# A routed feed-forward stage whose first tiles are fetched in four steps instead of two

## Chip, cores and metric

One core of one Trainium2 chip. The time is device microseconds of one execution; the median of three runs of the kernel before is 184.93 us (184.1 to 185.01). Everything below names lines of the kernel before.

## What is computed

Three layers, each closed by a residual sum and a layer norm, on 1,024 tokens (4 sequences of 256) of width 256, in fp32.

```python
x = _layernorm(x + attn(x, Wq, Wk, Wv, Wo))        # 16 heads that share one softmax
x = _layernorm(x + xattn(x, token_ids, ctx))       # expert = token_id // 3125, of 4
x = _layernorm(x + ffn(x, Wr, br, Wg, Wu, Wd))     # expert = argmax of a router, of 4

# ffn: each token goes to one expert e
h = silu(x @ Wg[e]) * (x @ Wu[e])                  # 256 -> 1024
y = (h @ Wd[e]) * top_probability                  # 1024 -> 256
```

Layers two and three both send each token to one of four experts, so the tokens are sorted by expert twice. The change is about the second sort, between layer two and layer three.

## The kernel before

**Layer two** works on ten tiles of 128 rows (T = 10). Its results are normalised in four groups (GROUPS: tiles 0 to 2, 3 and 4, 5 and 6, 7 to 9). For each group VectorE picks the expert of every row (`choose`), TensorE adds up how many earlier rows go to each expert (`rank`, into the PSUM tile `pR`), VectorE turns that into a row number (`place`), and GpSimd scatters each tile's rows to a buffer in DRAM, `scr2`, by that number (`scatter2`). There every expert has a region of eight blocks of 128 rows.

**Layer three** works on items (q, t): a quarter q of the hidden width and a tile t. A tile is one block of one expert. The last tile (JOINT = 9) joins two half blocks of up to 64 rows, of two experts, in one. There are 4 x 10 items, and in the first quarter tile and item have the same number. For an item j TensorE transposes the rows of a tile (`ftx`, L819), multiplies by the gate and up weights (`fup`, L833; each fp32 product is made from three fp32r products of high and low parts, L574), transposes the hidden rows (`fth`, L877) and multiplies by the down weights (`fdown`, L885). ScalarE copies the high parts (`fxhi`, `fhhi`) and does the silu (`fsilu`), VectorE makes the low parts (`fxlo`, `fhlo`), the product of gate and up (`fhidden`) and adds up the result (`fsum`). Each engine goes through a list written out in program order; for a usual i it is `ftx(i+1)`, `fup(i)`, `fth(i-1)`, `fdown(i-2)`. Nothing overtakes on an engine.

**Which block is a tile** is found out at run time. A block that is sure to be full can be worked on before all rows are scattered: with n tiles routed at least (128 n - 4 x 127) / 128 blocks, rounded up, are full. The kernel before uses this once. After seven routed tiles (ROUTED = 7, the first three groups) VectorE looks for three full blocks (EARLY = 3; `early_whole`, `early_table`, L1364 to L1371), which become tiles 0 to 2. The other full blocks, the larger rests and the smaller rests get tiles 3 to 9 after all ten tiles (`late_counts`, `late_blocks`, `late_rows`, L1378 to L1391).

VectorE hands on two kinds of numbers by semaphore. `row_table` (L1350) tells SyncE's DMA queue where a tile begins in `scr2`; SyncE reads each number into a register (`first_row`, L390) and starts the load (`routed_row`, L393). `tables` (L1361) tells TensorE which expert's weights a tile needs; TensorE reads that into a register at the head of each `fup` (L830). `late_offsets` (L1393) ends with `joint_expert`, the two experts of the joint tile; SyncE waits for it (L416), reads two registers, loads their weights of the first quarter in fp32 (`load_w32`, L409: two DMAs of 768 KB each) and then the two halves of the joint tile's rows (L419 to L421).

**SyncE's order before**, around the change (L395 to L425): wait for `row_table` 1, three register reads, wait for seven scatters, load tiles 0 to 2; wait for `row_table` 2, three reads, wait for the last three scatters, load tiles 3 to 5; wait for `row_table` 3, read and load tiles 6, 7 and 8; wait for `row_table` 4, `load_w32(0)`, the joint rows; then the weight chunks 7 to 15 (`load_chunk`, 768 KB each), each when a staging slot is free.

**The weights of the next quarter** are split beside the items: ScalarE copies a piece of 128 x 512 as high part (L964), GpSimd subtracts (L487). `share` (L312) says how many of 12 pieces go beside each item, and item 10, the first of the second quarter, waits for all twelve. Chunk 7 holds the last three pieces of that quarter.

Between the layers TensorE runs products of ones that nobody reads (`idle_products`, L582: 20 before the last `rank`, 6 behind it, 2 behind `ftx(0)` and `ftx(1)`).

Of the kernel before, what the change touches and what calls it, by code (L numbers as in the profile page):

```python
# [16 lines left out]
P = 128  # L17
# [6 lines left out]
E = 4  # L24
# [30 lines left out]
LATE = 2 * EARLY  # L55
SORTED = BATCH - 1
ROUTED = 7
# [10 lines left out]
def route_kernel(nc, aw, xT_in, x_in, ids_in, wr_in, br_in, ctx_in, ctxn_in, wffn_in, out):  # L68
# [3 lines left out]
    with ExitStack() as ctx:  # L72
# [57 lines left out]
        base8 = sb("base8", [P, T + 2, E + 1], BF16)  # L130
# [11 lines left out]
        slot_of = sb("slot_of", [P, BLOCKS])  # L142
        shift = sb("shift", [P, BLOCKS + 1])
# [74 lines left out]
        pR = bank[6][:, 0:(T + 2) * (E + 1)].rearrange("p (t e) -> p t e", e=E + 1)  # L218
# [12 lines left out]
        d_scat1, d_scat2, d_out = [sem(f"d_scat1_{i}") for i in range(2)], [sem(f"d_scat2_{i}") for i in range(2)], sem("d_out")  # L231
# [80 lines left out]
        share = [[0, 0, 1, 1, 2, 2, 2, 2, 2, 0], [1, 1, 2, 1, 2, 1, 2, 1, 1, 0], [1, 1, 2, 1, 2, 1, 2, 1, 1, 0]]  # L312
# [9 lines left out]
        CONSTS = 27  # L322
# [8 lines left out]
        def _(sp):  # L331
# [99 lines left out]
        def _(pool):  # L431
            def const(ins):
# [30 lines left out]
                         allow_small_or_imprecise_dtypes=True))  # L463
            const(g.memset(cap[:], HIGH))
            const(g.iota(base8[:, :, 0:E], pattern=[[0, T + 2], [REGION // P, E]], base=0, channel_multiplier=0,
# [62 lines left out]
            def scatter2(t):  # L528
                pool.wait_ge(slot_ready, GROUP_OF[t] + 1)
                pool.wait_ge(x2_ready, t + 1)  # L530
                g.indirect_dma_start(out=scr2, out_offset=bass.IndirectOffsetOnAxis(ap=slot2[:, t:t + 1], axis=0),  # L531
                                     in_=buf[:, t, :], in_offset=None, bounds_check=E * REGION - 1,
                                     oob_is_err=False).then_inc(d_scat2[t // ROUTED], 16)

# [16 lines left out]
            for t in range(ROUTED, T):  # L551
                scatter2(t)
# [18 lines left out]
        def _(pe):  # L571
# [207 lines left out]
            def rank(n):  # L779
                a, b = GROUPS[n]  # L780
                pe.wait_ge(mask_ready, n + 1)
                mm(pR[:, a:b, :], below[:], m2[:, a:b, :], start=False, stop=False, skip_group_check=True)
                for s in range(a, b):
                    end = T + 2 if s < ROUTED else T + 1
# [30 lines left out]
            idle_products(20)  # L815
            rank(3)
            idle_products(6)
# [81 lines left out]

            pe.wait_ge(tables, 2)  # L900
            ftx(0)
            for i in range(len(items) + 2):
                if i == EARLY:
                    fth(i - 1)
                    fdown(i - 2)
                    ftx(i)
                    ftx(i + 1)
                    fdown(i - 1)
                    pe.wait_ge(tables, 3)
                    fup(i)  # L910
                else:
                    if i + 1 < JOINT and i + 1 != EARLY:
                        ftx(i + 1)
                    if i == 0:
                        idle_products(2)
                    if i < len(items):
                        fup(i)
                    if i + 1 == JOINT:
                        ftx(i + 1)
                    if 1 <= i <= len(items):  # L920
                        fth(i - 1)
                    if i >= 2 and i != EARLY + 1:
                        fdown(i - 2)
# [3 lines left out]
        def _(act):  # L927
# [138 lines left out]
            for t in range(ROUTED, T):  # L1066
                norm2(t)

# [27 lines left out]

            fxhi(0)
            for i in range(len(items) + 4):
                if i == EARLY:
                    fhhi(i - 1)  # L1100
                    fxhi(i)
                    fxhi(i + 1)
                    fsilu(i)
                else:
                    if i + 1 < JOINT and i + 1 != EARLY:
                        fxhi(i + 1)
                    if i < len(items):
                        fsilu(i)
                    if i + 1 == JOINT:
                        fxhi(i + 1)  # L1110
                    if 1 <= i <= len(items):
                        fhhi(i - 1)
                if i - 4 >= len(items) - T:
                    norm_row(i - 4 - (len(items) - T))
                if i < len(items):
                    for k in pieces_beside(i):
                        split(k)
# [3 lines left out]
        def _(dve):  # L1121
# [242 lines left out]
            def early_whole():  # L1364
                dve.wait_ge(r_done, GROUP_OF[ROUTED - 1] + 1)
                step(v.tensor_tensor(out=by_expert(whole[:]), in0=per_block(pR[:, T + 1, 0:E]), in1=ends[:], op=ALU.is_ge))

            def early_table():
                running(nth[:], whole[:])
                block_table(0, EARLY, 0, nth[:], BLOCKS)  # L1370
                row_table_of(0, EARLY)  # L1371

            def early_offsets():
                dve.wait_ge(row_table, 1)
                expert_table(0, EARLY)
                offset_table(0, EARLY)

            def late_counts():  # L1378
                counts = per_block(pR[:, T, 0:E])
                step(v.tensor_tensor(out=by_expert(by_size[:, 0, :]), in0=counts, in1=begins_half[:], op=ALU.is_gt))  # L1380
                step(v.tensor_tensor(out=by_expert(by_size[:, 1, :]), in0=counts, in1=begins[:], op=ALU.is_gt))
                step(v.tensor_tensor(out=by_size[:, 1, :], in0=by_size[:, 1, :], in1=by_size[:, 0, :], op=ALU.subtract))
                step(v.tensor_tensor(out=by_size[:, 0, :], in0=by_size[:, 0, :], in1=flags[:, 0, :], op=ALU.subtract))
                running(nth_by_size[:], by_size[:].rearrange("p s j -> p (s j)"))

            def late_blocks(a, b):
                block_table(a, b, a - EARLY, nth_by_size[:], 2 * BLOCKS)

            def late_rows(a, b):
                wrapped(a, b)  # L1390
                row_table_of(a, b)  # L1391
# [24 lines left out]
            for i in range(T):  # L1416
# [27 lines left out]
                if i == 9:  # L1444
                    shifts(2)
                    choose(2)
                    residual_sum(7)
            place(2)
            residual_moments(7)
            early_whole()  # L1450
            early_table()
# [78 lines left out]
            for i in range(len(items) + 3):  # L1530
                if i == EARLY:
                    fhlo(i - 1)
                    fxlo(i)
                    fxlo(i + 1)
                    fhidden(i)
                else:
                    if 1 <= i and i + 1 < JOINT and i + 1 != EARLY:
                        fxlo(i + 1)
                    if i == 1:
                        late_blocks(LATE, MOST)  # L1540
                    if i < len(items):
                        fhidden(i)
                    if i + 1 == JOINT:
                        fxlo(i + 1)
                    if 1 <= i <= len(items):
                        fhlo(i - 1)
                if i == 1:
                    late_rows(LATE, MOST)
                    late_offsets()
                if 2 <= i <= len(items) + 1 - T:  # L1550
# [50 lines left out]
```

## Time and profile before

| | |
|---|---|
| median of 3 runs | 184.93 us (184.1 to 185.01) |
| the profiled execution, own time | 185.8 us |
| its span, first to last instruction | 184.0 us |
| TensorE busy | 168.6 us (92%) |
| VectorE, ScalarE, GpSimd busy | 122.9, 93.4, 106.0 us |
| granted TensorE clock, mean | 0.988 |
| chain that ended last, TensorE's share | 73% |
| the same, GpSimd | 10% |

The profiled execution took 1.8 us more than its span, and 0.9 us more than the median. Times in rows are us from the start of the span. Matmuls overlap, so a row's duration is longer than the distance to the next row; costs on TensorE are therefore read as distances between starts. Register reads and DMA issues do not count as busy time, and rows of SPq are the DMA queue's own.

### The profile page before, as it was taken

How to read it: one execution, taken by the hardware profiler on the slowest of the kernel's cores; microseconds unless marked ns; L12 is line 12 of the kernel's file. 1: busy time of each engine (PE TensorE's matmuls, PEld its weight loads, DVE VectorE, ACT ScalarE, POOL GpSimd, SP SyncE). 2: the span in 40 equal slices, each digit the busy share in tenths (PEclk: the TensorE clock that was granted, in tenths of full speed). 3: DMA queues.
4: the chain of work that ended last, by engine and by line, in shares of the span. 5: the costliest groups of instructions: out<-in, count | busy, mean ns of one | idle time of the engine just before them, and what ended most of it. 6: DMA issues, size and time to landing. Idle time of an engine off the chain costs nothing.

```text
span 184.0 us, 3730 instructions
## 1 busy us (share of the span) xinstructions
PE 168.6 (92%) x947; PEld 125.4 (68%) x947; DVE 122.9 (67%) x398; ACT 93.4 (51%) x244; POOL 106.0 (58%) x128
## 2 busy tenths in 40 slices
PE   7999998859999999999999999999999999999810
PEld 2778766337877745778867788867888677867600
DVE  3489688849687777746555364444799867877840
ACT  2268979416466632428763466635666421354430
POOL 8101666632928665126997999934688600367683
PEclk9999999999999999999999999999999999999995
DMA  4999998257999623249756275652860005311010
GB/s 136 368 316 420 381 392 335 75 149 204 361 337 388 229 90 99 79 121 321 234 206 241 98 303 187 215 191 100 269 246 0 4 0 195 151 57 57 25 66 28
DMA packets 14405, 35.30 MB, mean 192 GB/s; under 512 B 1838, under 2 KB 8112, under 8 KB 14258
## 3 DMA queue, kind: packets, MB, share of 16 engines
q1 hardware_dynamic: 12752, 31.84, 49.9%
q0 software_dynamic: 1344, 3.22, 4.8%
q8 instruction: 10, 0.16, 0.4%
q14 instruction: 9, 0.07, 0.1%
q10 hardware_dynamic: 290, 0.01, 0.1%
HBM read 26.44 MB, written 8.88 MB: 192 GB/s over the span
## 4 chain that ended last, share of the span: by engine, by line
PE 73%; POOL 10%; DVE 4%; DMA 4%; issue 4%; ACT 2%; POOLq 1%; SPq 0%; DVEq 0%; ACTq 0%
PE bank L576 12%; PE bank L577 11%; PE bank L578 11%; POOL w_lo L487 7%; PE bank L584 6%; PE bank L774 4%; PE bank L737 4%; PE bank L882 4%; PE bank L861 3%; PE bank L647 3%; PE bank L678 2%; DMA x_sorted<-buf,slot 2%; PE bank L872 2%; PE bank L590 2%; POOL out_tokens L565 2%
## 5 line engine op out<-in xcount | busy, mean ns | idle before, releaser
L487 POOL TENSOR_TENSOR w_lo<-stage,w_hi 128x512 fp32r<-128x512 f32 x40 | 50.8, 1298 | 24.6 <-ACT w_hi L964 18.1
L1080 ACT ACTIVATE gate<-bank 128x256 f32<-128x256 f32 x40 | 15.4, 384 | 48.5 <-PE bank L578 42.3
L1472 DVE TENSOR_TENSOR hid<-bank,gate 128x256 f32<-128x256 f32 x40 | 17.0, 425 | 30.0 <-ACT gate L1080 29.7
L576 PE MATMUL bank<-w_hi,xr 128*128 x72 | 29.7, 412 | 1.0 <-DVE xr L1405 0.6
L577 PE MATMUL bank<-w_lo,xr 128*128 x72 | 28.4, 394 | 0.0
L578 PE MATMUL bank<-w_hi,xr 128*128 x72 | 28.3, 393 | 0.0
L491 POOL TENSOR_TENSOR rstd<-mv,mhalf 128x1 f32<-128x1 f32 x18 | 10.9, 605 | 28.8 <-DVE mv L1218 28.6
L964 ACT ACTIVATE w_hi<-stage 128x512 fp32r<-128x512 f32 x45 | 26.9, 631 | 0.9 <-PE bank L578 0.9
L576 PE MATMUL bank<-w_hi,hT 128*128 x72 | 23.3, 324 | 0.7 <-DVE hT L1480 0.7
L578 PE MATMUL bank<-w_hi,hT 128*128 x72 | 20.3, 282 | 0.0
L577 PE MATMUL bank<-w_lo,hT 128*128 x72 | 20.3, 282 | 0.0
L576 PEld LDWEIGHTS bank<-w_hi,xr 128*128 128x128 f32 x72 | 13.6, 189 | 5.4 <-issue 3.6
L882 PEld LDWEIGHTS bank<-ident,hid 128*128 128x128 f32 x80 | 10.6, 139 | 8.2 <-issue 3.2
L584 PE MATMUL bank<-ones 128*128 128x512 bf16 x54 | 14.8, 426 | 1.1 <-POOL ones L437 1.1
L882 PE MATMUL bank<-ident,hid 128*128 128x128 f32 x80 | 15.6, 276 | 0.1
L578 PEld LDWEIGHTS bank<-w_hi,xr 128*128 128x128 f32 x72 | 13.5, 188 | 3.0
L531 POOL DMA_INDIRECT x_sorted<-buf,slot x10 | 10.1, 1008 | 9.1 <-DVE slot L1334 6.5
L1480 DVE TENSOR_TENSOR hT<-bank,hT 128x256 fp32r<-128x256 f32 x36 | 15.0, 416 | 0.3 <-ACT hT L1088 0.3
L577 PEld LDWEIGHTS bank<-w_lo,xr 128*128 128x128 f32 x72 | 13.6, 189 | 1.5
L576 PEld LDWEIGHTS bank<-w_hi,hT 128*128 128x128 f32 x72 | 13.7, 190 | 1.3 <-issue 1.3
L565 POOL DMA_INDIRECT out_tokens<-buf,outidx x10 | 10.3, 1030 | 6.9 <-ACT buf L1094 4.4
L1088 ACT ACTIVATE hT<-bank 128x256 fp32r<-128x256 f32 x36 | 13.7, 380 | 0.6 <-PE bank L882 0.6
(228 smaller groups left out, 344.1 us busy)
## 6 DMA issues: line engine op xcount, KB each, us to landing
stage<-in_w_ffn SPq DMA_DIRECT2D x15, 768.0 KB, 4.4
arena<-in_w_ffn SPq DMA_DIRECT2D x8, 768.0 KB, 4.9
rows<-x_sorted SPq DMA_DIRECT2D x19, 132.0 KB, 2.2
x_sorted<-xr SPq DMA_DIRECT2D x2, 1056.0 KB, 7.6
x_sorted<-xr SPq DMA_DIRECT2D x1, 1584.0 KB, 14.1
buf<-in_x_tok SPq DMA_DIRECT2D x1, 1024.0 KB, 11.8
w_hi<-in_ctx SPq DMA_DIRECT2D x1, 1024.0 KB, 11.5
w_hi<-in_ctxT SPq DMA_DIRECT2D x1, 1024.0 KB, 14.6
```

Source lines behind the costliest of these rows:

```text
L487: g.tensor_tensor(out=lo, in0=src, in1=hi.bitcast(F32), op=ALU.subtract).then_inc(split_lo, 1)
L565: g.indirect_dma_start(out=out, out_offset=bass.IndirectOffsetOnAxis(ap=outidx[:, t:t + 1], axis=0), in_=buf[:, t, 0:D], in_offset=None, b ...
L576: mm(dst, xhi, whi, start=start, stop=False)
L577: mm(dst, xhi, wlo, start=False, stop=False)
L578: return mm(dst, xlo, whi, start=False, stop=stop)
L584: mm(bank[2][:, :].rearrange("p (a b) -> p a b", a=4), ones[:], idle_rhs, start=True, stop=True)
L882: last = tr(fH[j % 2][:, k * P:(k + 1) * P], hid[:, (T + j) % 2, k * P:(k + 1) * P], ident[:])
L964: a(hi, src, ACT.Copy).then_inc(split_hi, 1)
L1080: a(gate[:, (T + j) % 2, :], fA[j % 2][:, 0:FQ], ACT.Silu).then_inc(silu_done, 1)
L1088: a(hT[:, j % 2, 0, :], fH[j % 2][:, 0:FQ], ACT.Copy).then_inc(hhi_done, 1)
L1472: v.tensor_tensor(out=hid[:, (T + j) % 2, :], in0=fA[j % 2][:, FQ:2 * FQ], in1=gate[:, (T + j) % 2, :], op=ALU.mult).then_inc(h_done, 1)
L1480: v.tensor_tensor(out=hT[:, j % 2, 1, :], in0=fH[j % 2][:, 0:FQ], in1=hT[:, j % 2, 0, :].bitcast(F32), op=ALU.subtract).then_inc(hlo_done, 1)
```

## The change

The second sort goes in four steps: tiles 0 and 1 are found and fetched after five routed tiles, tile 2 after seven, tile 3 after eight, the others after all ten. For this `pR` and `base8` get two more groups of running counts, four semaphores in place of two count the scatters, and the items 0 to 4 are written out by hand on TensorE, ScalarE and VectorE instead of coming from the loop. On SyncE, tile 6 is loaded behind `row_table` 5, and tiles 7 and 8 come behind `row_table` 6 and the two loads of `load_w32(0)`. The three `norm2` of the last group are interleaved with `fxhi` on ScalarE. The idle products become 14 before `ftx(0)`, 3 before the last `rank` and 2 before `fup(0)`. One piece of the weight split moves from item 8 to item 1.

```diff
-LATE = 2 * EARLY
+FIRST2, THIRD, FOURTH = 2, 3, 4
+LATE = 6
-ROUTED = 7
+ROUTED = [5, 7, 8, T]
+STAGE_OF = [sum(t >= n for n in ROUTED) for t in range(T)]
...
-        share = [[0, 0, 1, 1, 2, 2, 2, 2, 2, 0], [1, 1, 2, 1, 2, 1, 2, 1, 1, 0], [1, 1, 2, 1, 2, 1, 2, 1, 1, 0]]
+        share = [[0, 1, 1, 1, 2, 2, 2, 2, 1, 0], [1, 1, 2, 1, 2, 1, 2, 1, 1, 0], [1, 1, 2, 1, 2, 1, 2, 1, 1, 0]]
...
# SyncE
             sp.wait_ge(row_table, 1)
-            r = [first_row(t) for t in range(EARLY)]
-            sp.wait_ge(d_scat2[0], 16 * ROUTED)
-            for t in range(EARLY):
-                routed_row(t, r[t])
+            r0 = first_row(0)
+            sp.wait_ge(d_scat2[0], 16 * ROUTED[0])
+            routed_row(0, r0)
+            routed_row(1, first_row(1))
             sp.wait_ge(row_table, 2)
-            r = [first_row(t) for t in range(EARLY, LATE)]
-            sp.wait_ge(d_scat2[1], 16 * (T - ROUTED))
-            for t in range(EARLY, LATE):
-                routed_row(t, r[t - EARLY])
+            r2 = first_row(2)
+            sp.wait_ge(d_scat2[1], 16 * (ROUTED[1] - ROUTED[0]))
+            routed_row(2, r2)
             sp.wait_ge(row_table, 3)
-            for t in range(LATE, JOINT):
-                routed_row(t, first_row(t))
+            r3 = first_row(3)
+            sp.wait_ge(d_scat2[2], 16 * (ROUTED[2] - ROUTED[1]))
+            routed_row(3, r3)
+            sp.wait_ge(row_table, 4)
+            r = [first_row(t) for t in range(FOURTH, LATE)]
+            sp.wait_ge(d_scat2[3], 16 * (ROUTED[3] - ROUTED[2]))
+            for t in range(FOURTH, LATE):
+                routed_row(t, r[t - FOURTH])
+            sp.wait_ge(row_table, 5)
+            routed_row(LATE, first_row(LATE))
...
-            sp.wait_ge(row_table, 4)
+            sp.wait_ge(row_table, 6)
             joint = [sp.value_load(joint_expert[0:1, h:h + 1], min_val=0, max_val=(E - 1) * P) for h in range(2)]
             load_w32(0)
+            for t in range(LATE + 1, JOINT):
+                routed_row(t, first_row(t))
...
# TensorE
-            idle_products(20)
-            rank(3)
-            idle_products(6)
+            idle_products(14)
...
+            ftx(0)
+            idle_products(3)
+            rank(3)
+            ftx(1)
             pe.wait_ge(tables, 2)
-            ftx(0)
-            for i in range(len(items) + 2):
-                if i == EARLY:
-                    fth(i - 1)
-                    fdown(i - 2)
-                    ftx(i)
-                    ftx(i + 1)
-                    fdown(i - 1)
-                    pe.wait_ge(tables, 3)
-                    fup(i)
-                else:
...
+            idle_products(2)
+            fup(0)
+            ftx(2)
+            fup(1)
+            fth(0)
+            fup(2)
+            fth(1)
+            fdown(0)
+            fth(2)
+            ftx(3)
+            fdown(1)
+            pe.wait_ge(tables, 3)
+            fup(3)
+            ftx(4)
+            fdown(2)
+            fth(3)
+            ftx(5)
+            fup(4)
+            for i in range(5, len(items) + 2):
+                if i + 1 < JOINT:
+                    ftx(i + 1)
+                if i == 6:
+                    pe.wait_ge(tables, 4)
+                if i < len(items):
+                    fup(i)
...
# VectorE, behind the last items of layer two
...
             variances(3)
-            early_offsets()
+            first_chosen()
+            penalties()
+            next_row(2, T + 2, GROUP_OF[ROUTED[1] - 1])
             shifts(3)
             choose(3)
+            early_offsets()
+            fxlo(0)
             place(3)
-            early_chosen()
-            late_counts()
-            fxlo(0)
+            next_chosen(2)
+            penalties()
             fxlo(1)
-            late_blocks(EARLY, LATE)
-            late_rows(EARLY, LATE)
+            next_row(3, T + 1, GROUP_OF[ROUTED[2] - 1])
+            next_chosen(3)
...
+            fhidden(0)
+            late_counts()
+            fxlo(2)
+            large_blocks()
+            fhidden(1)
+            row_table_of(FOURTH, LATE)
+            fhlo(0)
+            middle_offsets()
+            fhidden(2)
+            fhlo(1)
+            late_order()
+            fhlo(2)
+            fxlo(3)
+            fsum(0)
+            late_rows()
+            fhidden(3)
+            fxlo(4)
+            fsum(1)
+            fhlo(3)
+            late_offsets()
+            fxlo(5)
+            fhidden(4)
+            fsum(2)
...
             def late_offsets():
-                dve.wait_ge(row_table, 3)
-                expert_table(EARLY, MOST)
-                offset_table(EARLY, JOINT)
+                dve.wait_ge(row_table, 5)
+                expert_table(LATE, MOST)
                 v.scalar_tensor_tensor(out=joint_expert[:], in0=expert[:, JOINT:MOST], scalar=float(P),
                                        in1=ones_f[:, 0:2], op0=ALU.mult, op1=ALU.mult).then_inc(row_table, 1)
+                offset_table(LATE, JOINT)
```

`late_rows` signals `row_table` 5. `next_row` finds the next full block in four small steps on 32 flags and signals `row_table` with a fifth:

```python
def next_row(t, row, group):
    c = t - FIRST2
    whole_of(row, group)
    step(v.scalar_tensor_tensor(out=next_key[:], in0=whole[:], scalar=-2.0 * BLOCKS, in1=penalty[:],
                                op0=ALU.mult, op1=ALU.add))
    step(v.tensor_reduce(out=next_of[:, c:c + 1], in_=next_key[:], axis=AX.X, op=ALU.min))
    step(v.scalar_tensor_tensor(out=block_no[:, t:t + 1], in0=next_of[:, c:c + 1], scalar=2.0 * BLOCKS,
                                in1=ones_f[:, 0:1], op0=ALU.add, op1=ALU.mult))
    row_table_of(t, t + 1)
```

## Rows read from the trace of the kernel before

**Rows 1.** Busy time by stretch: us, PE, PEld, DVE, ACT, POOL, clock, DMA share, GB/s.

```profile
98.40:171.00 72.60, 72.59 (x426) 57.02 (x427) 48.77 (x131) 34.03 (x87) 45.68 (x36) 1.00 0.39 138
```

**Rows 2.** Timeline of PE: start, us, line, operation; the first product of each step.

```profile
72.26 0.49 PE L576 MATMUL bank<-w_hi,xr 128*128 x1 [0.33 <-DVE xr L1405]
...
81.21 0.49 PE L576 MATMUL bank<-w_hi,xr 128*128 x1 [0.29 <-DVE xr L1405]
...
84.78 0.49 PE L576 MATMUL bank<-w_hi,xr 128*128 x1
...
86.28 0.38 PE L882 MATMUL bank<-ident,hid 128*128 128x128 f32 x2
...
87.22 0.38 PE L825 MATMUL bank<-ident,rows 128*128 128x128 f32 x2
87.35 0.48 PE L576 MATMUL bank<-w_hi,xr 128*128 x1
...
98.41 0.49 PE L576 MATMUL bank<-w_hi,xr 128*128 x1 [0.37 <-POOL w_lo L487]
```

**Rows 3.** Timeline of POOL, 54 to 90 us: the scatters of tiles 4 and 6.

```profile
63.10 0.97 POOL L531 DMA_INDIRECT x_sorted<-buf,slot  x1 [0.30 <-ACT buf L1041]
...
65.78 0.97 POOL L531 DMA_INDIRECT x_sorted<-buf,slot  x1 [0.30 <-issue]
```

**Rows 4.** Timeline of SP's DMA queue, 56 to 90 us.

```profile
68.40 12.47 SPq L393 DMA_DIRECT2D rows<-x_sorted  x9
82.20 1.29 SPq L414 DMA_DIRECT2D arena<-in_w_ffn  x2
84.25 1.82 SPq L421 DMA_DIRECT2D rows<-x_sorted  x2
87.08 0.34 SPq L338 DMA_DIRECT2D stage<-in_w_ffn  x1
```

**Rows 5.** Line L393, the loads of tiles' rows: time to landing.

```profile
DMA to landing us min/median/max: 2.0/2.1/2.3
```

**Rows 6.** Timeline of DVE, 54 to 90 us.

```profile
68.74 0.18 DVE L1325 TENSOR_TENSOR m<-at_max 128x15 bf16<-128x15 f32 x1
...
69.63 0.18 DVE L1148 SCALAR_TENSOR_TENSOR flags<-nth,whole 128x32 f32<-128x32 f32 x1
69.84 0.19 DVE L1380 TENSOR_TENSOR by_size<-bank,begins_half 128x32 f32<-128x32 f32 x1
...
77.84 0.15 DVE L1397 SCALAR_TENSOR_TENSOR joint_expert<-expert,ones_f 128x2 int32<-128x2 f32 x1
```

**Rows 7.** The page's costliest groups: high and low part of the hidden rows; busy, mean ns.

```profile
L1480 DVE TENSOR_TENSOR hT<-bank,hT 128x256 fp32r<-128x256 f32 x36 | 15.0, 416 | 0.3 <-ACT hT L1088 0.3
...
L1088 ACT ACTIVATE hT<-bank 128x256 fp32r<-128x256 f32 x36 | 13.7, 380 | 0.6 <-PE bank L882 0.6
```

**Rows 8.** Line L830, TensorE's read of an offset, 71 to 72.2 us: ns, start.

```profile
L830 PEldq TENSOR_LOAD <-off x1: 306/306/306, 71.1 to 71.1; - x1
```

**Rows 9.** Line L417, SyncE's two reads for the joint tile: ns, first and last start.

```profile
L417 SPq TENSOR_LOAD <-joint_expert x2: 268/270/271, 80.9 to 81.5; - x2
```

**Rows 10.** DMA in 84.3 to 87.2 us, in 87.2 to 88.9; the load at 84.25.

```profile
DMA packets 216, 1.23 MB, mean 424 GB/s; under 512 B 16, under 2 KB 16, under 8 KB 216
...
DMA packets 225, 0.44 MB, mean 257 GB/s; under 512 B 48, under 2 KB 176, under 8 KB 225
...
rows<-x_sorted SPq DMA_DIRECT2D x1, 66.0 KB, 4.3
```

**Rows 11.** Timeline of POOL, 78 to 99 us: the last ten pieces before item 10.

```profile
85.76 12.50 POOL L487 TENSOR_TENSOR w_lo<-stage,w_hi 128x512 fp32r<-128x512 f32 x10 [0.60 <-ACT w_hi L964]
```

**Rows 12.** The page's DMA issues: a weight chunk, KB, median us to landing.

```profile
stage<-in_w_ffn SPq DMA_DIRECT2D x15, 768.0 KB, 4.4
```

**Rows 13.** TensorE's last product, and the stretch in which its clock fell.

```profile
175.05 0.28 PE L578 MATMUL bank<-w_hi,hT 128*128 x1
...
179.00:180.00 1.00, 0.00 (x0) 0.00 (x0) 0.00 (x0) 0.60 (x1) 1.00 (x1) 0.80 0.09 33
```

More of the change, by code:

```diff
@@ L550, in _ @@
             pool.wait_ge(d_init2[3], 32)
-            for t in range(ROUTED, T):
+            for t in range(GROUPS[3][0], T):
                 scatter2(t)
@@ L1095, in norm_row, with splits_beside @@
                   scale=rstd[:, n % 2, 0:1]).then_inc(out_ready, 1)
+            def splits_beside(i):
+                for k in pieces_beside(i):
+                    split(k)
+            norm2(7)
             fxhi(0)
-            for i in range(len(items) + 4):
-                if i == EARLY:
-                    fhhi(i - 1)
[L1101 to L1112, printed above, removed]
+            norm2(8)
+            fxhi(1)
+            norm2(9)
+            fsilu(0)
+            fxhi(2)
+            fsilu(1)
+            fhhi(0)
+            splits_beside(0)
+            splits_beside(1)
+            fsilu(2)
+            fhhi(1)
+            fhhi(2)
+            fxhi(3)
+            splits_beside(2)
+            fsilu(3)
+            fxhi(4)
+            fhhi(3)
+            fxhi(5)
+            splits_beside(3)
+            fsilu(4)
+            splits_beside(4)
+            for i in range(5, len(items) + 4):
+                if i + 1 < JOINT:
+                    fxhi(i + 1)
+                if i < len(items):
+                    fsilu(i)
+                if i + 1 == JOINT:
+                    fxhi(i + 1)
+                if i <= len(items):
+                    fhhi(i - 1)
                 if i - 4 >= len(items) - T:
@@ L1362, in offset_table, with whole_of @@
                                        op0=ALU.mult, op1=ALU.mult).then_inc(tables, 1)
[L1364 to L1371, printed above, removed]
+            def whole_of(row, group):
+                dve.wait_ge(r_done, group + 1)
+                step(v.tensor_tensor(out=by_expert(whole[:]), in0=per_block(pR[:, row, 0:E]), in1=ends[:], op=ALU.is_ge))
@@ new lines, in first_whole, with first_table, first_chosen, penalties @@
+            def first_whole():
+                whole_of(T + 3, GROUP_OF[ROUTED[0] - 1])
+            def first_table():
+                block_table(0, FIRST2, 0, nth[:], BLOCKS)
+                row_table_of(0, FIRST2)
+            def first_chosen():
+                step(v.scalar_tensor_tensor(out=chosen[:], in0=nth[:], scalar=float(FIRST2), in1=whole[:],
+                                            op0=ALU.is_le, op1=ALU.mult))
+            def penalties():
+                step(v.scalar_tensor_tensor(out=penalty[:], in0=chosen[:], scalar=2.0 * BLOCKS, in1=block_at[:],
+                                            op0=ALU.mult, op1=ALU.add))
@@ L1373, in early_offsets, with next_chosen @@
+            def next_chosen(t):
+                c = t - FIRST2
+                step(v.scalar_tensor_tensor(out=chosen[:], in0=next_key[:], scalar=next_of[:, c:c + 1], in1=chosen[:],
+                                            op0=ALU.is_equal, op1=ALU.add))
             def early_offsets():
-                dve.wait_ge(row_table, 1)
-                expert_table(0, EARLY)
-                offset_table(0, EARLY)
+                dve.wait_ge(row_table, 2)
+                expert_table(0, THIRD)
+                offset_table(0, THIRD)
@@ L1378, in late_counts @@
             def late_counts():
                 counts = per_block(pR[:, T, 0:E])
-                step(v.tensor_tensor(out=by_expert(by_size[:, 0, :]), in0=counts, in1=begins_half[:], op=ALU.is_gt))
+                step(v.tensor_tensor(out=by_expert(whole[:]), in0=counts, in1=begins_half[:], op=ALU.is_gt))
                 step(v.tensor_tensor(out=by_expert(by_size[:, 1, :]), in0=counts, in1=begins[:], op=ALU.is_gt))
-                step(v.tensor_tensor(out=by_size[:, 1, :], in0=by_size[:, 1, :], in1=by_size[:, 0, :], op=ALU.subtract))
@@ L1383, in late_counts @@
-                step(v.tensor_tensor(out=by_size[:, 0, :], in0=by_size[:, 0, :], in1=flags[:, 0, :], op=ALU.subtract))
-                running(nth_by_size[:], by_size[:].rearrange("p s j -> p (s j)"))
[L1386 to L1391, printed above, removed]
+                step(v.tensor_tensor(out=by_size[:, 0, :], in0=whole[:], in1=chosen[:], op=ALU.subtract))
@@ new lines, in large_blocks, with middle_offsets, late_order @@
+            def large_blocks():
+                running(nth[:], by_size[:, 0, :])
+                block_table(FOURTH, LATE, 0, nth[:], BLOCKS)
+            def middle_offsets():
+                dve.wait_ge(row_table, 4)
+                expert_table(THIRD, LATE)
+                offset_table(THIRD, LATE)
+            def late_order():
+                step(v.tensor_tensor(out=by_size[:, 1, :], in0=by_size[:, 1, :], in1=whole[:], op=ALU.subtract))
+                running(nth_by_size[:], by_size[:].rearrange("p s j -> p (s j)"))
@@ L1447, in _ @@
                     residual_sum(7)
+            running(nth[:], whole[:])
             place(2)
+            first_table()
             residual_moments(7)
-            early_whole()
-            early_table()
             evicted_stats(8)
@@ L1528, in finish_norm @@
                                        in1=rstd[:, t % 2, 0:1], op0=ALU.mult, op1=ALU.mult).then_inc(nmr_ready, 1)
-            for i in range(len(items) + 3):
-                if i == EARLY:
-                    fhlo(i - 1)
[L1533 to L1550, printed above, removed]
+            fhidden(0)
[21 more added lines that the diff above has]
+            fsum(2)
+            for i in range(5, len(items) + 3):
+                if i + 1 < JOINT:
+                    fxlo(i + 1)
+                if i < len(items):
+                    fhidden(i)
+                if i + 1 == JOINT:
+                    fxlo(i + 1)
+                if i <= len(items):
+                    fhlo(i - 1)
+                if i <= len(items) + 1 - T:
                     fsum(i - 2)
```

47 lines of the change are left out of this document (25 added, 22 removed).

## Prediction

> **What bounds the kernel.** I read the page's busy shares first, then busy time by stretch, then the timelines of one engine at a time around the second sort. Once layer three runs steadily TensorE has no gaps: 72.59 of 72.60 us from 98.4 to 171.0 [rows 1]. So a shift of item 10 (the first of the second quarter) shifts the end by the same amount, unless something makes a new gap later. Only what comes before item 10 is in question. In [rows 2] the first product of item 0 starts at 72.26, of item 3 at 81.21, of item 5 at 84.78, of item 6 at 87.35 and of item 10 at 98.41; the last one waited 0.37 us for GpSimd's weight pieces, so TensorE by itself would have been there at 98.04. The same rows give the step lengths: a `fup` takes 1.50 (84.78 to 86.28), `fth` and `fdown` together 0.94 (86.28 to 87.22), an `ftx` 0.13.
>
> **Part 1: item 0 starts earlier.** Tile 0 now needs the scatters of tiles 0 to 4, not 0 to 6. The last of these starts at 63.10 and not at 65.78 [rows 3]. Before, the load followed the scatter by 68.40 - 65.78 = 2.62 [rows 3, 4], so it now goes out at 65.7 and lands 2.1 later [rows 5], at 67.8. That does not set the start of item 0, because `tables` 2, which was signalled early before, now covers three tiles and stands behind `choose(3)`. `choose(3)` ended at 68.92 [rows 6]. Four more small steps than before stand ahead of it; a step costs 0.21 (69.63 to 69.84, rows 6), so 0.84 in all. Much of this falls in the wait for GpSimd's root or was made free by work moved ahead of `place(2)`; I take 0.1, bounds 0 and 0.84. Three steps of `early_offsets` (0.63) bring `tables` 2 to 69.65. TensorE reads the offset behind that. The read of before began at 71.1 and the product came at 72.26 [rows 2, 8], 1.15 at most. Item 0 starts at **70.8**, a gain of 1.5.
>
> **Part 2: items 1 to 5.** Items 0 to 3 took 81.21 - 72.26 = 8.95. `fdown(2)` and one `ftx`, 0.81 + 0.13, move behind `fup(3)`, so item 3 starts at 70.8 + 8.0 = **78.8**, 2.4 earlier. The lookups for tiles 2 to 5 on VectorE are more steps than before, and some stand ahead of `fxlo(2)` and `fhidden(2)`; before there were as many in these places (the joint table of eight tiles), so I set them at 0, bounds -0.5 and +0.6. Then TensorE has `fup(3)` 1.50, `fdown(2)` and `fth(3)` 0.94, three `ftx` 0.39 and `fup(4)` 1.50, together 4.3, and one register read that is behind a wait and not hidden, 1.15 at most. Item 5 starts at about **84.2**, against 84.78. Most of the gain is gone by here: what was won at item 3 is spent on `fdown(2)`, which before had been done, and on the read.
>
> **Part 3: tiles 7 and 8 come late.** This is where I expect the loss. Before, `row_table` 3 served tiles 6 to 8, and the nine row loads were all issued in 12.47 us from 68.40, by 80.87 [rows 4]. `joint_expert` was ready at 77.99 [rows 6], so the two weight loads of the joint tile went out behind the rows, at 82.20. Now tiles 7 and 8 stand behind `row_table` 6 and behind those two loads. `row_table` 6 is signalled in `late_offsets`, which on VectorE stands behind `fhlo(3)`. `fhlo(3)` needs `fth(3)`: 78.8 + 1.50 + 0.13 + 0.81 = 81.25. Then come 0.13 for it and about 0.2 of hand-over, ScalarE's copy of 0.38 and VectorE's low part of 0.42 [rows 7], and three steps of 0.21: 83.0. SyncE reads two registers; from the first read at 80.9 to the weight load at 82.20 [rows 4, 9] it was 1.3. So the weights go out at **84.3**, 2.1 later than before.
>
> What the loads of tile 7 meet is read from what the joint tile's rows met, which stood in that place before. Their first load went out at 84.25 and took 4.3 us [rows 4, 10], against 2.1 for a load of twice the bytes with a free queue [rows 5]. From 84.3 to 87.2 the engines moved 216 packets, of which the 16 under 2 KB are all under 512 B [rows 10]: no packet of a row, only weights. The rows' packets, over 512 B and under 2 KB, appear from 87.2 on (176 - 48 = 128, rows 10), and the load lands at 88.55. The queue is worked off in order. Tile 7 therefore lands at 88.55 + 2.1 = **90.6**. TensorE has finished `fdown(3)` at 84.2 + 1.50 + 0.94 = 86.6, and its next step is `ftx(7)`, past which nothing can go. After it comes 0.13 and the register read of item 6, which waits in the same program order, some 0.8 (under the 1.15 above). Item 6 starts at 91.5, against 87.35: 4.15 later. Tile 8 and the joint tile land right behind, before they are needed.
>
> From item 6 to item 10 the work is the same: 98.04 - 87.35 = 10.7, so item 10 starts at 102.2 and not at 98.41, **3.8 later**. GpSimd is not what ends last any more: chunk 7 is issued behind the rows, at 87.08 + 3.2 = 90.3 (two more reads and loads of about 1.1 each, and 2.1 later, less the wait for a slot it had), lands 4.4 later [rows 12] at 94.7, and its three pieces at 12.50 / 10 = 1.25 each [rows 11] are done near 99.
>
> **Edits set at nothing.** A further index row among GpSimd's constants and the wider running counts lie beside TensorE's products of ones; their cover is the wait of TensorE for VectorE, and without it they would cost 0.2. The products of ones themselves are fewer, in a wait. `norm2` of tile 9 stands behind two copies, which makes the last scatters 0.5 later and with them tiles 4 and 5; these are needed only from 80 on. The piece moved from item 8 to item 1 fills GpSimd earlier; it could bring at most the 0.37 of [rows 2], which is hidden behind the stall.
>
> **The sum:** +3.8 on the profiled execution's 185.8 us is 189.6; that execution was 0.9 above the median of 184.93, so I forecast 184.93 + 3.8 = **188.7 us**.
>
> **Rivals.** (a) *The clock falls in the new stall.* TensorE would be idle from 86.6 to 90.6. After the last product at 175.05 (end 175.33) its granted clock went from 1.00 to a mean of 0.80 in the slice from 179 to 180 [rows 13], the lower level of 1.2 GHz, some 4 us or more after the engine had stopped. The stall is just about as long. Each item worked at the lower level would cost up to another 2.5 us (the 2.57 from 84.78 to 87.35 once more); I take one: 191.2. The Trainium skill, "TensorE: Matmul & The Clock Gate", section "Part 1: The HAM clock gate", says that an idle array is throttled to half and that sustained work releases it; the fall at the end of this trace agrees, but no row here has work at the lower level. (b) *The rows do not queue behind the weights.* Against it are [rows 10]; for it, that these loads are whole tiles and not halves. Tile 7 would be issued 84.25 - 82.20 = 2.05 after the weights, at 86.35, land at 88.45, and item 6 would start at 89.5: +2.2 less 0.37, 186.7. (c) *Tile 7 is there in time but chunk 7 is late*, because SyncE's list is longer: item 10 at about 99.1, +0.7, 185.6. (d) *Faster.* VectorE gets to `late_offsets` some 4 us earlier than I work out, so that tile 7 lands before TensorE asks for it and chunk 7 with it. The point that decides is tile 7's landing at 86.8. Then the 0.6 at item 5 and the 0.37 stay won: 184.0 or a little less. For it speaks that `row_table` 5 and 6 hang on few steps; against it that program order puts them behind `fhlo(3)`, and that behind item 3. That the change does not do what it says is no rival: five routed tiles hold at least 640 - 508 = 132 rows in full blocks, so two blocks, and the orders are fixed.
>
> **Chances.** Forecast 0.58, (a) 0.14, (b) 0.12, (c) 0.07, (d) 0.09. Below 0.5% (0.9 us) this kernel's measurement can't tell a change from none, so slower is forecast, (a) and (b): 0.84, same is (c): 0.07, faster (d): 0.09. The forecast's own range is 187.6 to 189.6, from the bounds of parts 1 and 2. The range with (a) and (b), 0.84 in all, is 186.2 to 191.3.
>
> **What would show it.** Right: item 0 at 70.8, item 3 near 78.8, the two fp32 weight loads near 84.3, a gap of about 4 us on TensorE ahead of the seventh pair of transposes with a row load as its releaser, tile 7's load taking over 4 us, item 10 near 102. Wrong: no gap ahead of `ftx(7)`, weight loads before 82, or a row load behind them that lands in 2 to 3 us.

## Result and profile after

The changed kernel takes **191.71 us** (median of 4 runs, 191.19 to 193.87) against 184.94 (184.1 to 185.01): 3.99% slower, ratio 1.0399, 95% interval 1.0311 to 1.0487. The forecast was 188.7, range 186.2 to 191.3. The direction is right, and so is the main term, the late load of tile 7 at 3.8 us. The size is not: part 2 of the prediction set the added lookups at 0, and the fall of the clock was left to a rival and not in the sum. The time lies just above the range. Ratios and their intervals go by undisturbed executions alone, so that a few runs below rest on fewer executions than they list.

Layer two ended at 63.83 in this execution, where the idle products begin, and at 64.57 before; I put the difference down to the first sort's scatters, which the change does not touch, but no run tests that. In the twelve profiles of this case that point lies anywhere from 62.86 to 64.57. Times after it are therefore compared as distances from it where tenths matter.

First TensorE's timeline of the changed kernel, with the same columns as [rows 2]. L594 is the first product of a `fup` or `fdown` (before L576), L841 an `ftx`.

```profile
63.83 3.19 PE L602 MATMUL bank<-ones 128*128 128x512 bf16 x14
...
70.13 0.49 PE L594 MATMUL bank<-w_hi,xr 128*128 x1
...
76.46 0.38 PE L594 MATMUL bank<-w_hi,hT 128*128 x1 [0.75 <-DVE hT L1562]
...
79.07 0.49 PE L594 MATMUL bank<-w_hi,xr 128*128 x1 [0.48 <-DVE xr L1483]
...
82.10 0.44 PE L898 MATMUL bank<-ident,hid 128*128 128x128 f32 x2 [0.45 <-DVE hid L1554]
...
86.10 0.44 PE L841 MATMUL bank<-ident,rows 128*128 128x128 f32 x2 [1.22 <-DMA rows<-x_sorted]
87.03 0.49 PE L594 MATMUL bank<-w_hi,xr 128*128 x1 [0.50 <-issue]
...
91.81 0.44 PE L841 MATMUL bank<-ident,rows 128*128 128x128 f32 x2 [2.21 <-DMA rows<-x_sorted]
92.66 0.79 PE L594 MATMUL bank<-w_hi,xr 128*128 x1 [0.41 <-issue]
...
104.67 0.40 PE L594 MATMUL bank<-w_hi,xr 128*128 x1
```

Item 0 starts at 70.13 (before 72.26), item 3 at 79.07 (81.21), item 5 at 87.03 (84.78), item 6 at 92.66 (87.35) and item 10 at 104.67 (98.41). The gain of two microseconds is there up to item 3 and gone at item 5. Two waits on row loads stand ahead of tiles 6 and 7: TensorE had run dry at 84.88 and at 89.60, and stood for 1.22 and 2.21 us. From item 10 to the end of the span it is 190.2 - 104.67 = 85.5 us, before 184.0 - 98.41 = 85.6: all of the loss lies ahead of item 10.

The next lines are SyncE's DMA queue, as in [rows 4]: the weights of the joint tile (L428) at 85.20, the loads of tiles 7 and 8 (the second L400 line) behind them.

```profile
66.00 16.80 SPq L400 DMA_DIRECT2D rows<-x_sorted  x7
85.20 0.85 SPq L428 DMA_DIRECT2D arena<-in_w_ffn  x2
86.80 1.43 SPq L400 DMA_DIRECT2D rows<-x_sorted  x2
88.99 1.84 SPq L437 DMA_DIRECT2D rows<-x_sorted  x2
```

The load at 86.80, tile 7's, asked for alone (its last column is us to landing):

```profile
rows<-x_sorted SPq DMA_DIRECT2D x1, 132.0 KB, 5.0
```

A load that takes 2.1 with a free queue [rows 5] took 5.0 behind 1.5 MB of weights. Tile 6's load, which left at 82.47 with nothing large ahead of it, took 3.6 in this execution, and that is its wait of 1.22:

```profile
rows<-x_sorted SPq DMA_DIRECT2D x1, 132.0 KB, 3.6
```

Why it was slow isn't shown. It did not set item 6: the chain that ended last (first column the start, second the length) goes around tile 6, through VectorE's lookups, SyncE's reads for the joint tile, the weights and the load of tile 7.

```profile
79.26 1.33 DVE arena L1382
...
83.92 0.28 SPq L431
...
85.20 0.33 SPq L428
...
86.80 4.97 DMA rows<-x_sorted
```

Two things I had not put in the sum. The first is in VectorE's timeline, and GpSimd's beside it:

```profile
74.74 1.25 DVE L1393 SCALAR_TENSOR_TENSOR row<-block_no,ones_f 128x2 int32<-128x2 f32 x1
...
79.18 1.40 DVE L1382 TENSOR_TENSOR arena<-nth_by_size,tile_no 128x320 f32<-128x320 f32 x1
```

```profile
74.69 1.28 POOL L505 TENSOR_TENSOR w_lo<-stage,w_hi 128x512 fp32r<-128x512 f32 x1 [0.26 <-ACT w_hi L991]
78.95 1.29 POOL L505 TENSOR_TENSOR w_lo<-stage,w_hi 128x512 fp32r<-128x512 f32 x1 [2.98 <-ACT w_hi L991]
```

A step on two columns takes 1.25 us and ends at 75.99; GpSimd's subtraction, begun 0.05 earlier, ends at 75.97. The second ends at 80.58, 0.34 behind the subtraction's end at 80.24. Both steps read two tiles in SBUF. The second thing is the clock, in busy time by stretch as in [rows 1]:

```profile
90.00:92.00 2.00, 0.19 (x2) 0.19 (x2) 0.22 (x1) 0.41 (x1) 2.00 (x2) 1.00 0.92 323
92.00:94.00 2.00, 1.59 (x5) 1.17 (x5) 0.42 (x1) 0.38 (x1) 0.46 (x1) 0.61 0.97 231
94.00:96.00 2.00, 2.00 (x8) 1.51 (x8) 0.00 (x0) 0.38 (x1) 0.00 (x0) 0.54 1.01 390
96.00:98.00 2.00, 2.00 (x14) 1.78 (x14) 1.41 (x4) 1.70 (x5) 0.99 (x1) 1.00 0.41 172
```

The seventh column is the granted clock: 1.00 until TensorE has stood in the stall, then 0.61 and 0.54, that is mostly 1.2 GHz, while item 6 runs, then 1.00 again.

### The profile page after: what moved, and what is told of

It is laid out like the page before. It is cut to its first block, busy times and chain, and to the rows that moved or that the text cites. A ratio compares the mean times of both kernels' runs of the same rounds, so it can differ in the third digit from the quotient of the medians.

```text
span 190.2 us, 3732 instructions
## 1 busy us (share of the span) xinstructions
PE 169.5 (89%) x938; PEld 126.0 (66%) x938; DVE 127.2 (67%) x414; ACT 93.8 (49%) x244; POOL 106.2 (56%) x129
## 4 chain that ended last, share of the span: by engine, by line
PE 70%; DVE 8%; DMA 8%; issue 5%; POOL 3%; ACT 1%; SPq 1%; POOLq 1%; DVEq 0%
PE bank L594 12%; PE bank L595 12%; PE bank L596 11%; DMA rows<-x_sorted 5%; PE bank L898 5%; PE bank L792 4%; PE bank L877 4%; DMA x_sorted<-buf,slot 3%; PE bank L602 3%; PE bank L755 3%; PE bank L665 3%; PE bank L608 3%; PE bank L696 2%; PE bank L888 2%; POOL out_tokens L583 2%
## 5 line engine op out<-in xcount | busy, mean ns | idle before, releaser
L594 PE MATMUL bank<-w_hi,xr 128*128 x72 | 30.1, 419 | 2.1 <-issue 1.4
L596 PE MATMUL bank<-w_hi,xr 128*128 x72 | 28.7, 399 | 0.0
L594 PE MATMUL bank<-w_hi,hT 128*128 x72 | 23.4, 325 | 1.5 <-DVE hT L1562 1.5
L594 PEld LDWEIGHTS bank<-w_hi,xr 128*128 128x128 f32 x72 | 13.8, 192 | 6.9 <-issue 5.2
L596 PEld LDWEIGHTS bank<-w_hi,xr 128*128 128x128 f32 x72 | 13.8, 192 | 3.2
L594 PEld LDWEIGHTS bank<-w_hi,hT 128*128 128x128 f32 x72 | 13.8, 191 | 2.1 <-issue 2.1
L595 PEld LDWEIGHTS bank<-w_lo,hT 128*128 128x128 f32 x72 | 13.8, 191 | 0.0
## 6 DMA issues: line engine op xcount, KB each, us to landing
buf<-in_x_tok SPq DMA_DIRECT2D x1, 1024.0 KB, 10.6
```

What stands on the lines that cost most here:

```text
L594: mm(dst, xhi, whi, start=start, stop=False)
L595: mm(dst, xhi, wlo, start=False, stop=False)
L596: return mm(dst, xlo, whi, start=False, stop=stop)
```

## Experiments

Three theories came out of this: A, tiles 7 and 8 stand behind the joint weights; C, GpSimd's subtraction keeps VectorE's step waiting ("the lock" below); D, the clock falls in the stall. Each was taken away alone, then together. "Distance" is from the start of the idle products behind layer two to the start of item 10, in the profiled execution; it is 98.41 - 64.57 = 33.84 before (the products begin at 64.57) and 104.67 - 63.83 = 40.84 after.

### The rows ahead of the weights

```diff
             sp.wait_ge(row_table, 5)
-            routed_row(LATE, first_row(LATE))
+            for t in range(LATE, JOINT):
+                routed_row(t, first_row(t))
...
             load_w32(0)
-            for t in range(LATE + 1, JOINT):
-                routed_row(t, first_row(t))
```

> The changed kernel with one thing undone: tiles 7 and 8 are loaded right behind tile 6, ahead of the joint tile's two weight loads. Theory A (the loss is mostly the place of tiles 7 and 8 in SyncE's list): tile 6's load went out at 82.5 in the changed kernel's trace, so tiles 7 and 8 go out near 83.6 and 84.7, there is no wait ahead of the transposes of tile 7 beyond the product before them, item 6 starts near 89.6 instead of 92.7 and at full clock, and the time falls by 3.1 + 1.3 = 4.4 us, to about 187.3. Rival B (chunk 7 of the next quarter, which stays behind the same loads, takes the place of the wait): item 10 still starts near 104 and the time falls by less than 1.5 us.

188.44 us (187.9 to 188.87), ratio to before 1.0209 (1.0172 to 1.0246); distance 37.2. The wait ahead of tile 7 is gone and the clock stays up, so A, with what hangs on it, is the largest part: 3.3 us. The 4.4 expected did not all come, for rival B (chunk 7) has a share. This is TensorE's and ScalarE's timeline of this kernel: the joint product (L876), and ScalarE's copies of two pieces of chunk 7.

```profile
97.82 1.94 PE L876 MATMUL bank<-arena 128*64 128x512 f32 x8 [2.18 <-issue]
```

```profile
95.65 1.15 ACT L990 ACTIVATE w_hi<-stage 128x512 fp32r<-128x512 f32 x2 [2.78 <-DMA stage<-in_w_ffn]
96.70 0.36 ACT L1103 ACTIVATE gate<-bank 128x256 f32<-128x256 f32 x1
96.97 0.27 ACT L1096 ACTIVATE arena<-bank 128x128 f32<-128x128 f32 x1
```

ScalarE stood for 2.78 us waiting for chunk 7, which left at 89.87 (before 87.08; 26.4 and 22.5 behind layer two's end). Queued behind that on ScalarE are the silu of item 8 and the copy of the joint tile's rows (L1096), and behind the copy TensorE's joint product. A transfer that is late for a piece not needed before item 10 held item 9 by 2.2 us, through the order of one engine.

### No weight pieces beside the lookups

```diff
-        share = [[0, 1, 1, 1, 2, 2, 2, 2, 1, 0],
+        share = [[0, 0, 0, 2, 2, 2, 2, 2, 2, 0],
```

> The changed kernel with the weight split of items 1 and 2 moved behind item 3 (0,0,0,2,2,2,2,2,2,0), so that GpSimd subtracts no piece while VectorE looks up tiles 4 to 9. 
190.89 us (190.69 to 191.8), ratio 1.0345 (1.0298 to 1.0391). No VectorE step of the lookups is longer than 0.5 us any more once no subtraction meets them, and the joint weights go out 20.62 behind the end of layer two (63.18 here) instead of 21.37:

```profile
83.80 0.85 SPq L428 DMA_DIRECT2D arena<-in_w_ffn  x2
85.40 1.43 SPq L400 DMA_DIRECT2D rows<-x_sorted  x2
```

```profile
83.72 0.49 PE L594 MATMUL bank<-w_hi,xr 128*128 x1 [0.16 <-issue]
...
90.40 0.44 PE L841 MATMUL bank<-ident,rows 128*128 128x128 f32 x2 [4.11 <-DMA rows<-x_sorted]
91.24 0.77 PE L594 MATMUL bank<-w_hi,xr 128*128 x1 [0.40 <-issue]
```

The time fell only by 0.8, under the 1.5 to 2.5 expected. Item 6 starts 28.06 behind layer two's end, 0.8 sooner than in the changed kernel and still 1.1 behind the forecast's 91.5 - 64.57 = 26.93; 0.5 of the lock's gain is lost at the front, where item 0 starts at 6.79 and not at 6.30, ahead of anything that the edit moves. TensorE now stands 4.1 us ahead of tile 7, and item 6 still runs at the low clock (a first product of 0.77 instead of 0.49).

### The clock held through the stall

```diff
             for i in range(5, len(items) + 2):
+                if i == 6:
+                    pe.wait_ge(h_done, T + 5)
+                    for _ in range(10):
+                        mm(bank[1][:, :].rearrange("p (a b) -> p a b", a=4), ones[:], idle_rhs, start=True, stop=True)
```

> The changed kernel with ten products of ones (2.2 us) put between the last down product before the stall and the transposes of tile 7. Nothing else moves. Theory D (about 1.3 us of the loss is item 6 running at the lower clock level after the stall): the granted clock stays 1.00 through the stall, item 6 takes 2.6 us instead of 4.0, and the time falls by 1.3 us, to 190.4. Rival (the clock falls all the same or is only a symptom): clock and time as in the changed kernel, 191.7.

191.18 us (190.18 to 191.7), ratio 1.0342 (1.029 to 1.0393). The granted clock is 1.00 in every stretch of the stall and behind it, and items 6 to 10 take 103.66 - 93.13 = 10.5 us, in the changed kernel 104.67 - 92.66 = 12.0. So the low clock costs 1.5 us. The time fell by 0.5 only; with the spread of the changed kernel's runs that is inconclusive by itself. In the profiled execution item 6 starts 0.4 later, measured from layer two's end, for tile 7 landed later. This profile also has both long VectorE steps (1.25 and 1.40), yet no wait for tile 6: its load took 2.0 us and TensorE went on at once.

```profile
84.31 0.41 PE L841 MATMUL bank<-ident,rows 128*128 128x128 f32 x2
```

So the lock alone did not bring the wait of 1.22 in the changed kernel.

### Lock and clock together

The two edits above in one kernel, with fourteen products.

> pieces_later with fourteen products of ones (3 us) in the stall ahead of tile 7, so that the lock and the clock are both gone and only the late tile 7 is left, which is what the forecast priced at 3.8 us. Expected: item 6 starts near 91.3 as in pieces_later but at full clock, item 10 near 102, and the time falls by 1.3 us to 189.5. Rival (the low clock was hidden by GpSimd's pieces, which end last before item 10): 190.9 as in pieces_later.

188.90 us (188.77 to 191.11), ratio 1.0252 (1.0183 to 1.0321). This is the changed kernel with only the late tile left, the one thing that the forecast priced, and it takes what the forecast said: 188.7. The distance is 101.48 - 63.62 = 37.9, against 33.84 + 3.8 = 37.6. Step by step, behind the end of layer two: item 0 at 6.1 (forecast 6.2), item 3 at 14.3 (14.2), item 5 at 19.7 (19.6), the joint weights at 20.0 (19.7), tile 7 at 26.4 (26.0), item 6 at 27.3 (26.9). Against `pieces_later`, items 6 to 10 took 10.6 us and not 12.2, which prices the low clock once more, at 1.6.

The parts do not add up: taken away one at a time they gave 3.3, 0.8 and 0.5, C and D together 2.8, and A and C together, below, all of it. The stall hangs on the lock, and the clock on the stall.

### The new order in the kernel before

```diff
             sp.wait_ge(row_table, 3)
-            for t in range(LATE, JOINT):
-                routed_row(t, first_row(t))
+            routed_row(LATE, first_row(LATE))
...
             load_w32(0)
+            for t in range(LATE + 1, JOINT):
+                routed_row(t, first_row(t))
```

> The kernel before, with only SyncE's new order: tiles 7 and 8 behind row_table 4 and behind the joint tile's two weight loads. There row_table 4 comes at 78.0. Theory A in full (the order costs only because row_table 6 comes late): the weights go out near 80.2, tile 7 lands near 86.5 behind them, TensorE asks for it at 87.2, so nothing waits and the time is 184.9 within 0.5. Rival (the order by itself costs what the change costs): a wait of 2 to 4 us ahead of tile 7 and 187 to 189 us.

185.73 us (184.99 to 186.93, 10 runs), ratio 1.0054 (1.0025 to 1.0082). The weights left at 79.62, tile 7 at 81.23, and it landed after 6.8 us at 88.03, a little behind TensorE's request for it, at 86.98:

```profile
88.03 0.44 PE L826 MATMUL bank<-ident,rows 128*128 128x128 f32 x2 [1.05 <-DMA rows<-x_sorted]
88.87 0.49 PE L577 MATMUL bank<-w_hi,xr 128*128 x1 [0.41 <-issue]
```

I had expected tile 7 at 86.5; the second weight load took 7.5 us to landing, 5.6 in the changed kernel. The profiled execution took 186.93, one of the three slowest of the ten. The order alone costs 0.8 us, not 3: it hurts in the changed kernel because the joint tile's experts are ready 20.06 behind the end of layer two there and 13.43 here, and the weights leave at 21.4 and 15.5.

### The lock in the kernel before

```diff
-        share = [[0, 0, 1, 1, 2, 2, 2, 2, 2, 0],
+        share = [[0, 1, 1, 1, 2, 2, 2, 2, 1, 0],
```

> The kernel before with only the new share list, so that one piece of the split goes beside item 1 and GpSimd subtracts it while VectorE looks up tiles 6 to 9. Theory C (lock): the VectorE step with two operands in SBUF that meets the subtraction (near 76.9) takes 1 us or more instead of 0.17, row_table 3, tables 3 and the product of item 2 come 1.2 us later, TensorE waits as much ahead of the transposes of item 2, and the time rises by 0.6 to 1.2 us, to 185.9 (part is hidden by GpSimd's pieces being earlier). Rival (no lock): no step grows, and the time stays or falls by up to 0.4 us.

186.81 us (186.32 to 187.36), ratio 1.0111 (1.006 to 1.0163): one moved piece of a split costs 1.9 us. VectorE, GpSimd and TensorE of this kernel:

```profile
76.35 1.19 DVE L1347 TENSOR_TENSOR block_no<-block_no,block_wrap 128x5 f32<-128x5 f32 x1
78.20 1.12 DVE L1361 SCALAR_TENSOR_TENSOR off<-expert,ones_f 128x6 int32<-128x6 f32 x1
```

```profile
76.22 1.29 POOL L487 TENSOR_TENSOR w_lo<-stage,w_hi 128x512 fp32r<-128x512 f32 x1 [2.66 <-ACT w_hi L964]
78.03 1.26 POOL L487 TENSOR_TENSOR w_lo<-stage,w_hi 128x512 fp32r<-128x512 f32 x1 [0.52 <-ACT w_hi L964]
```

```profile
79.78 0.69 PE L882 MATMUL bank<-ident,hid 128*128 128x128 f32 x2 [2.10 <-DVE hid L1472]
```

Two steps of a few columns, met by two subtractions, take 1.19 and 1.12 instead of 0.17. The second piece met one because the first had made VectorE late. TensorE stands 2.1 us for the product of item 2, where 1.2 was expected, and its clock falls to a mean of 0.60 in the 4 us behind. That is the lock with nothing else of the change, and the fall of the clock behind it.

### Both places mended, and what then is left

Rows ahead of the weights and no early pieces, in one kernel; timed twice, the second time in five rounds.

> The changed kernel with both edits that were tried one by one: tiles 7 and 8 loaded ahead of the joint tile's weights, and no piece of the weight split before item 3. Theory (place in SyncE's list and the lock of VectorE by GpSimd are together what the change costs): tiles 7 and 8 go out near 82 and 83, nothing waits for them, the joint weights go out near 84.5, chunk 7 near 88 and lands near 93, where ScalarE may wait for it by up to 1 us; item 10 starts near 98.5 as in the kernel before and the time is 185.3, within 0.8. Rival (something else in the four-step sort costs too): 187 or more.

> The same kernel as rows_first_pieces_later, timed in more rounds and on the same chip as chunk_first. Expected: 185.5, within 0.4, item 10 at 99.5.

185.46 us (184.36 to 187.05), ratio 1.0044 (0.9973 to 1.0116), and 184.65 us (184.1 to 187.48, 12 runs), ratio **1.0007** (0.9977 to 1.0036). The loss is gone, and no gain has come. In the second profile item 10 starts at 96.97, 34.1 us behind the end of layer two at 62.86, where the kernel before has 33.8; in the first, of the execution that took 187.05, it is 35.5. The joint product still waits, by 1.28 us there and 2.74 in the first profile, behind ScalarE's wait for chunk 7.

Two trials to win more failed. `late_offsets` right behind `fhidden(3)`:

> As rows_first_pieces_later, and late_offsets (four small steps that end in row_table 6 and tables 4) stands right behind fhidden(3) on VectorE, ahead of fxlo(4), fsum(1) and fhlo(3). row_table 6 comes about 1.2 us sooner, and with it the joint weights and chunk 7; fxlo(4) comes 0.6 later, which TensorE's register read for item 4 hides. If chunk 7 is what ends last before item 10 in rows_first_pieces_later, the time falls by 0.5 to 1 us below it, to 184.5. Rival (TensorE by itself or GpSimd's twelve pieces end last): no difference.

Ratio 1.002 (0.9945 to 1.0096), 184.66 to 188.47 us in four runs: nothing that can be measured. The joint tile's experts were ready 1.2 us sooner, as expected (17.43 behind the end of layer two for 18.65), but the joint weights left no sooner (20.74 for 20.59): SyncE was still reading and loading tiles 6 to 8, until 19.4. And chunk 7 ahead of the joint weights:

> rows_first_pieces_later with chunk 7 (the last weights of the second quarter) loaded ahead of the joint tile's fp32 weights. In rows_first_pieces_later's trace ScalarE waited 3.3 us for chunk 7, whose load went out at 88.0 behind 1.7 MB of joint weights and rows, and TensorE's joint product waited 2.7 us behind that. Theory (what is left of the loss is chunk 7's place in the queue): it now goes out when its slot is free, near 86.3, and lands near 90.6; the joint weights go out near 87 and land near 93; the joint product starts near 95, GpSimd's twelve pieces end near 98 and item 10 starts near 98.1 instead of 99.5, so the time falls to 184.2, a little below the kernel before. Rival (the joint weights become the late load): the joint product waits as long as before and the time stays at 185.5.

186.08 to 190.48 us, median 189.98 of 6, five of them at 188.96 or more; no ratio is given. The profile, of the one at 188.96, shows the rival: chunk 7 left at 85.85 and ScalarE no longer waited, but the joint tile's rows, now behind 2.3 MB, held TensorE.

```profile
95.86 0.56 PE L841 MATMUL bank<-ident,rows 128*128 128x128 f32 x2 [3.60 <-DMA rows<-x_sorted]
```

The DMA engines were busy for 91% or more of every stretch of 2 us from 88 to 98. In both orders that were tried, the load that goes last is the late one.

## Why the forecast was right and where it failed

**Part 1** was right: item 0 gained 2.13, of which 0.74 is layer two's earlier end, so 1.4 against 1.5.

**Part 2** failed. It set the added lookups at 0, with bounds -0.5 and +0.6, on the ground that there were as many steps before. The count was fair, since with the lock and the fall of the clock away items 3 and 5 start within 0.1 us of the forecast. What runs beside the lookups was left out: the change also moved a piece of the split to item 1 and stretched the lookups into the next piece. I had written of that piece that it "fills GpSimd earlier" and priced it at a gain. It cost 1.1 + 0.9 us of VectorE's time, and the joint tile's experts were ready at 20.06 and not at the forecast's 83.0 - 64.57 = 18.4 (18.67 with the lock away). The Trainium skill, "SBUF — State Buffer", section "SBUF: two separate sides", has the rule that would have shown it: a VectorE operation with two inputs in SBUF and a GpSimd operation that reads SBUF exclude each other for the whole instruction. The traces agree, with 1.25 and 1.40 for 0.16 and 0.48, and with 1.19 and 1.12 in the kernel before with one moved piece. VectorE's products and differences with an operand in PSUM went on beside GpSimd at 0.42.

**Part 3** was right in place and size: with the lock away and the clock held, tile 7 landed within 0.4 us of the forecast and item 6 started within 0.3.

**Rival (a)** happened; I had given it 0.14. I took a stall of 4 us to be "just about as long" as the idle time at the end of the trace. In the changed kernel TensorE stood for 2.2 us ahead of tile 7, and the clock fell all the same, so the comparison that I drew was not the right one. The fall cost 1.5 us. I had priced one item at half clock at 2.5, an upper end. The Trainium skill, "TensorE: Matmul & The Clock Gate", section "Part 1: The HAM clock gate", says that an idle array is throttled and sustained work releases it; the rows at 92 to 98 us agree.

**The sum of the miss**, from the end of layer two: item 6 at 28.83 against 26.93, so 1.9, and items 6 to 10 in 12.0 instead of the forecast's 10.7, so 1.3 for the clock. Together 3.2, which makes a distance of 37.6 + 3.2 = 40.8. Of the 1.9, 1.6 goes when the lock does (27.26, of which 0.2 is an earlier item 0), and 0.3 is part 3's own error. The range lacked a case with both. The forecast's own range was also added up wrong: the bounds of parts 1 and 2 give 188.1 to 190.0 and not 187.6 to 189.6, which would not have held 191.7 either.

**Why the change brought nothing even when mended.** It starts item 0 1.6 us earlier (6.1 for 7.7), but item 10 needs twelve pieces and the joint tile, and both hang on the end of SyncE's list. SyncE works through it from the row numbers of tiles 6 to 8 on. These came 12.7 us behind the end of layer two before and 16.0 here, since more lookups stand ahead of them, between more of the items' work; the joint weights left at 17.6 before and 20.6 here. `joint_sooner` shows that it is this and not the last lookup, since there the experts came sooner and the weights did not. What was won at the front was a wait; what bounds the stage then is the list of loads. Whether the four-step lookup has a cheaper order was not tried.

## What to carry over

A lookup that starts work sooner is paid for in what comes last: after such a change read when the last numbers are signalled, and what queue and which engine's program order stand behind them. Small transfers that an engine waits for go ahead of large ones on the same queue, since 132 KB took 5.0 us behind 1.5 MB and 2.1 alone. Before placing GpSimd work "beside" VectorE, look at whether VectorE's operands there are both in SBUF.

## What was unexpected of the hardware

VectorE steps of two to six columns took 1.1 to 1.25 us when they met a GpSimd subtraction of 128 x 512, seven times their own 0.16. The waits of 2.2 us in the changed kernel and of 2.1 us in the kernel before with one piece moved were followed by a stretch at the lower clock. Others of the same length were not: 2.4 us behind ten idle products in `clock_held`, and 2.2 and 2.7 us ahead of the joint product in `rows_first` and the first profile of `rows_first_pieces_later`, all with a granted clock of 1.00 behind them. So the length of one wait does not tell whether the clock falls, and what does isn't shown here.
